# A written-out ending for the last two batches of a fused adaLN transformer block

## The reference

```python
h = layernorm(x) * (1 + ca) + sa
x = x + ga * attention(h)       # 16 heads of 64, causal softmax, out @ Wo + bo
h = layernorm(x) * (1 + cb) + sb
x = x + gb * ffn(h)             # fp4(silu(fp4(h) @ fp4(Wg).T) * (fp4(h) @ fp4(Wu).T)) @ fp4(Wd).T
```

## Time and profile before

| | |
|---|---|
| median of three runs | 1296.12 us |
| profiled execution, its own time | 1295.38 us |
| its span, first to last instruction | 1293.6 us |
| mean granted TensorE clock | 0.989 |
| PE, DVE, ACT, POOL busy, share of the span | 96%, 76%, 69%, 66% |
| PE busy in the last of 40 slices | 3 tenths (7 in the one before, 9 in all but the first) |

### The profile page before, as it was taken

How to read it: one execution, slowest core, us unless ns; L and a number is a source line. 1 busy time by engine, 2 the same in 40 slices (tenths; PEclk the granted TensorE clock), 3 DMA queues, 4 the chain that set the end, 5 groups by cost and what they waited for, 6 DMA issues and landing times.

```text
span 1293.6 us, 34330 instructions
## 1 busy us (share of the span) xinstructions
PE 1247.5 (96%) x10194; PEld 1023.9 (79%) x10194; DVE 985.3 (76%) x2461; ACT 898.1 (69%) x2988; POOL 853.9 (66%) x1595
## 2 busy tenths in 40 slices
PE   6999999999999999999999999999999999999973
PEld 4778888888888878888878888888888888888853
DVE  5577877777878777878777877777787777787863
ACT  6776776777776777766777777777677777677640
POOL 4757676667676666766666766667766666767653
PEclk9999999999999999999999999999999999999995
DMA  3000000000000000000000000000000000000000
GB/s 104 20 20 24 18 6 23 22 22 22 16 10 18 22 22 22 20 6 18 22 22 22 22 11 11 22 22 22 22 16 6 22 22 22 22 16 6 19 20 10
DMA packets 38920, 26.53 MB, mean 21 GB/s; under 512 B 2896, under 2 KB 34128, under 8 KB 38896
## 3 DMA queue, kind: packets, MB, share of 16 engines
q1 hardware_dynamic: 38480, 25.96, 7.1%
q10 hardware_dynamic: 416, 0.26, 0.1%
HBM read 21.94 MB, written 4.28 MB: 20 GB/s over the span
## 4 chain that ended last, share of the span: by engine, by line
PE 94%; DVE 2%; ACT 2%; POOL 1%; issue 1%; DMA 0%; POOLq 0%; DVEq 0%; ACTq 0%
PE ps_m L1037 25%; PE ps_s L1136 19%; PE ps_m L1011 18%; PE ps_o L1166 14%; PE ps_m L1089 9%; PE ps_s L1146 5%; PE ps_m L1113 3%; ACT probs L659 1%; ACT qk L617 0%; DVE neg_max L861 0%; POOL qy L75 0%; POOL qy L73 0%; POOL probs L451 0%; DMA x_in<-L_attn_x 0%; POOL hq L77 0%
## 5 line engine op out<-in xcount | busy, mean ns | idle before, releaser
L659 ACT ACTIVATE probs<-ps_s,neg_max 128x128 f32<-128x128 f32 (+1 forms) x1024 | 424.1, 433 | 182.1 <-PE ps_s L1146 180.5
L451 POOL TENSOR_SCALAR probs<-probs,r_den 128x256 f32<-128x256 f32 (+1 forms) x768 | 354.9, 479 | 0.0
L861 DVE TENSOR_REDUCE neg_max<-ps_s 128x4 f32<-128x1024 f32 x256 | 305.6, 1215 | 61.1 <-PE ps_s L1136 61.1
L449 POOL TENSOR_TENSOR probs<-probs,r_den 128x128 f32<-128x128 f32 x256 | 107.3, 419 | 308.0 <-DVE r_den L872 293.8
L1136 PE MATMUL ps_s<-qk 64*128 64x256 f32 x2048 | 265.0, 394 | 1.8 <-ACT probs L659 1.8
L613 ACT COPY probs_t<-ps_m 128x512 f32<-128x512 f32 x288 | 168.5, 606 | 120.8 <-PE ps_m L1011 120.6
L1011 PE MATMUL ps_m<-ident,probs 128*128 128x128 f32 x1536 | 235.8, 277 | 7.1 <-ACT qk L617 3.6
L1136 PEld LDWEIGHTS ps_s<-qk 64*128 64x128 f32 x2048 | 183.0, 187 | 61.7 <-issue 32.5
L659 ACT ACTIVATION_READ_ACCUMULATOR probs<-ps_s,neg_max 128x1 f32 x1024 | 221.0, 216 | 0.0
L1011 PEld LDWEIGHTS ps_m<-ident,probs 128*128 128x128 f32 x1536 | 172.2, 140 | 40.4 <-ACT qk L617 13.4
L1166 PE MATMUL ps_o<-probs_t,v 128*64 128x256 f32 (+1 forms) x2048 | 194.7, 332 | 3.6 <-ACT probs_t L613 1.9
(11 more groups left out here) (111 smaller groups left out, 1787.6 us busy)
## 6 DMA issues: line engine op xcount, KB each, us to landing
mod_a<-mod_rows SPq DMA_DIRECT2D x32, 256.0 KB, 3.4
x_res<-L_attn_x SPq DMA_DIRECT2D x32, 128.0 KB, 2.1
out<-y_out SPq DMA_DIRECT2D x32, 128.0 KB, 1.8
x_in<-L_attn_x SPq DMA_DIRECT2D x31, 128.0 KB, 2.1
mod_b<-mod_rows SPq DMA_DIRECT2D x32, 64.0 KB, 2.9
wkv<-L_attn_Wkv SPq DMA_DIRECT2D x3, 256.0 KB, 6.0
wo<-L_attn_Wo SPq DMA_DIRECT2D x1, 512.0 KB, 5.6
wkv<-L_attn_Wkv SPq DMA_DIRECT2D x2, 128.0 KB, 3.7
```

Of the source, the lines that this page charges most:

```text
L449: nc.gpsimd.tensor_tensor(cols, cols, r_den[:, u % 4, 0:1].to_broadcast([P, P]), ALU.mult)
L451: ins = nc.gpsimd.tensor_scalar(cols, cols, r_den[:, u % 4, s:s + 1], 1.0, ALU.mult, ALU.mult)
L659: ins = nc.scalar.activation(probs[:, u % 4, h, t * P:(1 + 2 * t) * P], ps_s[:, 2 * (u % 2) + h, t * N:t * N + (1 + t) * P], ACT.Exp, bias ...
L861: nc.vector.tensor_reduce(neg_max[:, u % 4, :], ps_s[:, 2 * (u % 2):2 * (u % 2) + 2, :].rearrange("p b (t j) -> p (b t) j", t=2), AX.X, AL ...
```

## The change

Iterations 32 and 33 are gone from PE, ACT, DVE and POOL (`for i in range(last, B)`); SP's `body` stops after 31. Behind iteration 31 each engine gets a list of its own (`LAST` = 31, `FORE` = 30). In it:

- `wo` is summed in pieces, as pairs come in: units 0 to 3 of tile 0 behind the values of pair 2, then units 0 to 5 of tile 1 and 4 to 5 of tile 0, and the last two units of each behind the copy of pair 3.
- The steps use `ps_s`, `ps_o` and `ps_m` each with a bank of its own choice.
- The high part of `xqt` is copied by ACT; DVE does the low part.
- Scale and shift (`h2a`, `h2`) of batch 31, the fp4 rounding of its input, and that of its hidden tile 1 are on DVE. POOL rounds the hidden tiles of batch 30 and tile 0 of batch 31, and makes `rstd` of batch 31 between the two tiles of batch 30.
- Batch 31's result goes to `x_in` and is stored tile by tile; its gate row comes from a tile of its own, `mod_last`, loaded early.

`shared_step` takes the destination instead of a bank number; nothing else of iterations 0 to 31 changes.

```diff
@@ sync
             iterations(sp, body, B - 2)
-            sp.wait_ge(stored, 16 * B)
+            sp.dma_start(mod_last[:, :], mod_rows[LAST, 4].partition_broadcast(P)).then_inc(mod_last_loaded, 16)
+            sp.wait_ge(down_scaled, 2 * FORE)
+            sp.dma_start(mod_b[:, :], mod_rows[FORE, 4].partition_broadcast(P)).then_inc(mod_b_loaded, 16)
+            sp.wait_ge(y_ready, 2 * LAST)
+            sp.dma_start(out_v[FORE], y_out[:, :, :]).then_inc(stored, 16)
+            for t in range(2):
+                sp.wait_ge(y_ready, 2 * LAST + t + 1)
+                sp.dma_start(out_v[LAST][:, t, :], x_in[:, t, :]).then_inc(stored, 16)
+            sp.wait_ge(stored, 16 * (B + 1))
@@ gpsimd
             iterations(pool, body)
+            normalize_unit(LAST, UNITS - 1)
...
+            round_hidden_half(FORE, 0)
+            rstd(LAST, ln2_pool, x1_steps, X1_STEPS * B, mv2, var2, rstd2)
+            round_hidden_half(FORE, 1)
+            round_hidden_half(LAST, 0)
@@ scalar
+            last_out_copy(2, ps_o[:, :])
+            last_transposed(0)
+            act.wait_ge(xqt_full, LAST)
+            nc.scalar.copy(xq_r[0][:, :], ps_m[0][:, 0:N]).then_inc(xqt_high, 1)
+            last_transposed(1)
+            last_tanh(FORE, 0, ps_s[:, 0, 0:I])
+            last_out_copy(3, ps_s[:, 3, :])
+            last_tanh(FORE, 1, ps_s[:, 2, 0:I])
+            last_hidden_copy(FORE, 0, ps_o[:, 0:IP])
+            act.wait_ge(xqt_full, B)
+            nc.scalar.copy(xq_r[0][:, :], ps_m[1][:, 0:N]).then_inc(xqt_high, 1)
+            last_tanh(LAST, 0, ps_s[:, 0, 0:I])
+            last_tanh(LAST, 1, ps_s[:, 2, 0:I])
...
@@ vector
+            last_gated(FORE, 0, ps_s[:, 0, 0:I])
+            last_hidden(FORE, 0, ps_s[:, 1, 0:I])
+            last_hidden_scales(FORE, 0)
+            last_attended(0)
+            last_attended(1)
+            dve.wait_ge(x1_steps, X1_STEPS * LAST + 2)
+            layer_norm_stats(x1, stats2, mv2, x1_steps, X1_STEPS * LAST + 2)
+            last_gated(FORE, 1, ps_s[:, 2, 0:I])
+            last_hidden(FORE, 1, ps_m[0][:, 0:I])
+            dve.wait_ge(ln2_pool, 2 * B)
+            normalized([xn2[:, t * P:t * P + P] for t in range(2)], x1, mv2, rstd2, xn2_ready)
...
+            nc.vector.tensor_tensor(h2a_v, xn2_v, both_tiles(mod_a[:, 2, :]), ALU.mult).then_inc(h2a_ready, 1)
...
+            nc.vector.tensor_tensor(h2_v, h2a_v, both_tiles(mod_a[:, 3, :]), ALU.add).then_inc(h2_ready, 1)
...
+            quantize_scales(nc, Steps(dve, xq_steps, QUANT_STEPS, LAST), h2, 2 * P // BLOCK, amax[0], scale[0], inverse[0])
+            quantize_magic(nc, Steps(dve, xq_steps, QUANT_STEPS, LAST, SCALE_STEPS), h2, 2 * P // BLOCK, inverse[0], qy[0],
+                           qm[0])
+            dve.wait_ge(xqt_full, LAST)
+            quantize_round(nc.vector, Steps(dve, xq_round, ROUND_STEPS, LAST), xq, 2 * P // BLOCK, scale[0], qy[0], qm[0])
+            last_down(FORE, 0, ps_m[2][:, 0:P], mod_b[:, :], (mod_b_loaded, 16 * LAST), x1_keep, y_out)
+            dve.wait_ge(xqt_high, 2)
+            nc.vector.tensor_tensor(xq_r[1][:, :], ps_m[1][:, 0:N], xq_r[0][:, :], ALU.subtract).then_inc(xqt_ready, 2)
+            last_hidden_scales(FORE, 1)
+            last_gated(LAST, 0, ps_s[:, 0, 0:I])
+            last_hidden(LAST, 0, ps_s[:, 1, 0:I])
+            last_hidden_scales(LAST, 0)
+            last_gated(LAST, 1, ps_s[:, 2, 0:I])
+            last_hidden(LAST, 1, ps_m[0][:, 0:I])
+            last_hidden_scales(LAST, 1)
+            dve.wait_ge(hqt_full, 2 * LAST)
+            quantize_round(nc.vector, Steps(dve, hq_round[1], ROUND_STEPS, LAST), hq[:, 1, :], I // BLOCK, scale[2], qy[2], qm[2])
+            last_down(FORE, 1, ps_o[:, 0:P], mod_b[:, :], (mod_b_loaded, 16 * LAST), x1_keep, y_out)
+            for k in range(2):
+                last_down(LAST, k, ps_s[:, k, 0:P], mod_last[:, :], (mod_last_loaded, 16), x1, x_in)
@@ tensor
+            last_values(2, ps_o)
+            shared_step("t", LAST, 9, ps_s[:, 0, :])
...
+            last_attended(0, range(0, 4))
...
+            shared_step("xqt", FORE, 0, ps_m[0])
+            shared_step("t", LAST, 10, ps_s[:, 1, :])
+            shared_step("t", LAST, 11, ps_s[:, 2, :])
...
+            shared_step("gate", FORE, 0, ps_s[:, 0, :])
...
+            shared_step("up", FORE, 0, ps_s[:, 1, :])
+            last_values(3, ps_s[:, 3, :])
...
+            last_attended(1, range(0, 6))
+            last_attended(0, range(4, 6))
+            pe.wait_ge(ot_ready, PAIRS * B)
+            last_attended(0, range(6, 8))
+            last_attended(1, range(6, 8))
+            shared_step("gate", FORE, 1, ps_s[:, 2, :])
+            shared_step("up", FORE, 1, ps_m[0])
+            shared_step("hqt", FORE, 0, ps_o)
+            pe.wait_ge(wo_scaled, 2 * B)
+            shared_step("down", FORE, 0, ps_m[2][:, 0:P])
+            shared_step("xqt", LAST, 0, ps_m[1])
... gate and up of both tiles of LAST
+            shared_step("hqt", FORE, 1, ps_s[:, 3, :])
+            shared_step("down", FORE, 1, ps_o)
+            shared_step("hqt", LAST, 0, ps_m[1])
+            pe.wait_ge(gated, 2 * LAST + 1)
+            shared_step("down", LAST, 0, ps_s[:, 0, :])
+            shared_step("hqt", LAST, 1, ps_s[:, 3, :])
+            pe.wait_ge(h_ready, 2 * LAST + 1)
+            shared_step("down", LAST, 1, ps_s[:, 1, :])
```

More of the change, by code:

```diff
@@ L145, in adaln_block @@
         mod_b = sb("mod_b", [P, P])
+        mod_last = sb("mod_last", [P, P])
         stats1 = sb("stats1", [P, 2, 6])
@@ L253, in adaln_block @@
         xqt_ready = sem("xqt_ready")
+        xqt_high = sem("xqt_high")
         tanh_ready = sem("tanh_ready")
@@ L307, in iterations @@
                 body(i)
-            for i in range(last, B + 2):
+            for i in range(last, B):
                 body(i)
@@ L372, in adaln_block @@
         POOL_SETUP = 7
+        LAST, FORE = B - 1, B - 2
+        BANK_LEFT = {}
+        for _, (kind, b, part, bank, _) in sorted(shared_steps(LAST).items()):
+            BANK_LEFT[bank] = (kind, b, part)
         block = ctx.enter_context(nc.Block())
@@ L724, in _, with last_out_copy, last_tanh, last_hidden_copy @@
             iterations(act, body)
+            def last_out_copy(pair, src):
+                act.wait_ge(o_full, PAIRS * LAST + pair + 1)
+                nc.scalar.copy(o_t[:, 2 * pair:2 * pair + 2, :], src.rearrange("p (u j) -> p u j", u=2)).then_inc(ot_ready, 1)
+            def last_tanh(b, k, src):
+                act.wait_ge(gate_full, 2 * b + k + 1)
+                act.wait_ge(gated, 2 * b + k - 1)
+                nc.scalar.activation(th[:, k, :], src, ACT.Tanh, scale=0.5).then_inc(tanh_ready, 1)
+            def last_hidden_copy(b, k, src):
+                act.wait_ge(hqt_full, 2 * b + k + 1)
+                nc.scalar.copy(hq_t[:, k, :], src).then_inc(hqt_ready, 1)
+            def last_transposed(g):
+                act.wait_ge(pt_full, 3 * PAIRS * LAST + 10 + g)
+                nc.scalar.copy(probs_t[:, 4 * g:4 * g + 4, :], ps_s[:, g, :].rearrange("p (c j) -> p c j", c=4)
+                               ).then_inc(pt_ready[g], 1)
+            last_out_copy(2, ps_o[:, :])
[11 more added lines that the diff above has]
+            last_tanh(LAST, 1, ps_s[:, 2, 0:I])
+            last_hidden_copy(FORE, 1, ps_s[:, 3, 0:IP])
+            last_hidden_copy(LAST, 0, ps_m[1][:, 0:IP])
+            last_hidden_copy(LAST, 1, ps_s[:, 3, 0:IP])
         @block.vector
@@ new lines, in last_attended @@
+            def last_attended(k):
+                dve.wait_ge(wo_full, 2 * LAST + k + 1)
+                dve.wait_ge(mod_a_loaded, 16 * B)
+                dve.wait_ge(kept, LAST)
+                nc.vector.tensor_tensor(attn[:, k, :], ps_m[1 + k][:, 0:P], mod_a[:, 0, :], ALU.mult).then_inc(wo_scaled, 1)
+                dve.wait_ge(wo_scaled, 2 * LAST + k + 1)
+                dve.wait_ge(xgb_ready, B)
+                nc.vector.tensor_tensor(x1[:, k, :], attn[:, k, :], x_gb[:, k, :], ALU.add).then_inc(x1_steps, 1)
@@ new lines, in last_down @@
+            def last_down(b, k, src, gate, loaded, kept_x, dst):
+                dve.wait_ge(down_full, 2 * b + k + 1)
+                dve.wait_ge(*loaded)
+                nc.vector.tensor_tensor(ffn[:, k, :], src, gate, ALU.mult).then_inc(down_scaled, 1)
+                dve.wait_ge(down_scaled, 2 * b + k + 1)
+                dve.wait_ge(kept, LAST)
+                dve.wait_ge(stored, 16 * FORE)
+                nc.vector.tensor_tensor(dst[:, k, :], ffn[:, k, :], kept_x[:, k, :], ALU.add).then_inc(y_ready, 1)
@@ L1237, in _, with last_values @@
             for place in ((2, 7), (3, 1), (3, 2)):
-                shared_step(*shared[place][0:4])
+                kind, b, k, bank, _ = shared[place]
+                shared_step(kind, b, k, ps_m[bank])
             iterations(pe, body)
+            def last_values(pair, dst):
+                for g in range(3):
+                    pe.wait_ge(pt_ready[g], PAIRS * LAST + pair + 1)
```

(19 more changed lines are left out.)

79 lines of the change are left out of this document (65 added, 14 removed).

## The result

The changed kernel takes 1283.5 us, the median of four runs (1283.06 to 1283.81), against 1296.14 for the kernel before (1295.63 to 1297.10): a ratio of 0.9901, 95% interval 0.9889 to 0.9912. The forecast was 1283.7. A repeat beside the last experiments gave 1283.08 (1283.01 to 1284.93).

The account below looks back on a forecast made before the run. The ending behind 1257.5 is bound by a chain of dependent steps, one engine at a time. Links laid along old times: 1291.36 - 1279.0 = 12.4 us gained, span 1281.2, profiled run 1283.0, median 1283.7; own range 1282.6 to 1285.0.

Parts of the forecast that it names:

- Start: Start of the ending, PE's values of pair 2: stays at 1243.5, as iterations 0 to 31 are untouched.
- Rival 4: Looped batches: `mod_last` shifts later SBUF tiles and slows them; from 0.44 us each the whole gain is gone; chance 0.04.
- PE up to `wo`: PE from values of pair 2: 9.1 us of work, little waiting; `wo` complete at 1252.5 and 1253.0, before 1257.71.
- Rival 2: PE ahead of `wo`: idle time of the first stretch stays, `wo` ends at 1256; +2.3, 1286.0 us; chance 0.14.
- Residual sums and statistics: DVE behind `wo`: POOL's rounding holds both residual sums, to 1253.65 and 1254.6, 0.8 lost; statistics end 1255.4.
- rstd to rounding: Batch 31's input: `rstd` 1256.5, scale and shift on DVE to 1258.05, rounding ends 1261.4; 11.0 us won so far.
- Hidden part: Batch 31's hidden tiles: DVE does batch 30 tile 1 first, to 1265.45; fp4 ends 1269.5 and 1273.6, rounding 1275.25.
- The end: Transposes 0.88, copy 0.48, last down 1.5 and DVE 0.62 us: last sum at 1279.0, before 1291.36.
- Rival 1: PE in the ending: the clock comes back to full level, saving 1.5 us, so 1282.2; chance 0.14.
- Rival 3: DVE beside POOL's roundings: POOL holds every DVE instruction that reads SBUF, some 2.6 net, 1286.3 us; chance 0.08.
- The hold: DVE instructions with two SBUF inputs, or scales on SBUF, end only behind a running POOL product; 1.4 us in all.

Follow-up runs that it names:

- the last experiments: Runs of the changed kernel plus extra matmuls on idle PE, some with `xqt` of batch 30 moved earlier; medians 1283.06, 1282.71 and 1282.53 us.
- the one profiled execution with fillers: Changed kernel plus 52 bf16 matmuls into an unused bank where PE idles; values of pair 2 to last DVE sum 34.51 us against 35.96, median 1283.06.
- the thin roundings: Changed kernel with POOL's last three roundings cut to three two-column instructions each; values of pair 2 to last DVE sum 34.27 us against 35.96.
- the kernel with batch 30 first: Changed kernel with DVE's scales and magic of batch 30 tile 1 ahead of batch 31's normalization; 1286.69 us (one run).
- the two kernels with late sums: Changed kernel with `wo` in whole sums behind pair 3, 1283.76 us; also with both roundings, scale and shift on POOL and one store, 1287.36 us.
- in the last: Changed kernel with `xqt` of batch 30 earlier and extra PE matmuls: 32, then 20 and 14, and four behind the last transposes; median 1282.53 us.

## Why the prediction was right

The time was right to 0.2 us, and partly by luck: the gain in the stretch was 11.85 us where I had 12.4. The profiled run of before lay 0.74 below its median and that of after only 0.2, and the start of the ending, which wanders by 2 us between profiles, fell within 0.02 us of the old one. The mechanism, a chain of links that the new order shortens, is what the trace shows. By steps:

- *Start.* 1243.5 as before. Rival 4, 0.44 us for each looped batch or more, did not happen.
- *PE up to `wo`.* Tile 1 complete at 1253.35, forecast 1253.0. Gate began at 1247.83, not 1247.7, since I had left out the handoff of 0.14 from the split to PE; the other 0.2 is spread over the groups behind it (gate and up took 1.13 to the next group where I had 1.05). Rival 2 (1256) did not happen. That the early units delay `xqt` was not in my list; it costs up to 0.4.
- *Residual sums and statistics.* Held by POOL as priced in kind. In size the first was 0.47 (I had 0.75), the second 0.78 (0.6 to 0.65). Last sum at 1254.82, forecast 1254.6.
- *rstd to rounding.* 1256.76, 1258.32, 1261.76; forecast 1256.5, 1258.05, 1261.4. The five moved DVE instructions took 0.42 to 0.43. The roundings on DVE and scale and shift are worth 2.12 and 0.67 by experiment, 2.3 and 0.7 by the forecast's own terms.
- *Hidden part.* First product at 1265.76, forecast 1265.45: DVE's other batch is in front of it, as said. For the holding of L55 and L62 the sum had 0.7 and 0.63 us in the two tiles, which is less than the 0.71 and 0.33, 1.04 together, that it read for the two instructions in the old trace. Measured were 0.44 and 0.48: L62 took 0.85 twice, as in the old trace, but L55 only 0.29 and 0.33, since it began just ahead of the end of a POOL product. The queue's pause of 0.1 between the two products, which I had left out, made up for part of that. Magic ends at 1273.81, forecast 1273.6.
- *The end.* 1279.49, forecast 1279.0. The terms that were too small: down takes 1.62 at the lower clock, not 1.5, and the last transposes stand behind the down of tile 0 in PE's queue (1275.71; their input was done at 1275.49).
- *Rival 1* did not happen: the second and third stretch had clocks of 0.69 and 0.50. Its price was near: the prediction has 1.5 (its four terms add up to 1.6), and the one profiled execution with fillers won 1.45, though by another sum: 0.27 on `xqt`, nothing from the gate, 0.47 up to the end of the last transposes, 0.71 on down. *Rival 3* falls with the thin roundings.
- *The hold.* By the forecast the sum would be 1.4 us lower without it; by the rows of the thin roundings it is about 1.0 on the chain, the difference lying in the holding of L55 and L62. The Trainium skill (GPSIMD Engine Reference, Key points) names two-port modes and two SBUF inputs as what contends with POOL. The two-input instructions here agree (0.29 up to 0.78, 0.52 to 0.85); L55 has one SBUF input, and no run here shows whether it is in a two-port mode.

## What to carry to other kernels

When a pipeline drains, give its last iterations lists of their own: the longest chain first in every queue, older batches in its gaps. Here that, with the banks it needs, was 8.5 of 11.85 us, more than moving work to faster engines (2.8) and splitting sums (0.5); the split store gave nothing. What the free banks alone are worth was not tried. Price a DVE instruction that is held by a running POOL product by where that product ends, and count only what the next link then really waits for. And measure an ending from a mark in its own trace, not by total time, when the part ahead of it wanders by more than the effect.

## What was not expected of the hardware

- The hold lasts until the POOL instruction has ended: a DVE sum of 128 columns ended at 1254.82, 0.14 behind POOL's product (1254.68); L62 ended at 1268.99, 0.37 behind (1268.62). In the kernel with batch 30 first, two normalizations of 0.61 grew to 2.12. In the changed kernel and that one the held instruction ended 0.14, 0.28 and 0.37 us behind POOL's at 128, 256 and 352 columns. In the other direction it showed once in each of the two kernels with late sums: a DVE sum of 0.29 began 0.03 ahead of a POOL product, which then took 1.05 instead of 0.93. That is not simply who begins first: the first of the two normalizations also began 0.05 ahead of a POOL product, and was held by it. What decides is open.
- Fillers on PE do not keep the granted clock at its upper level (2.4 GHz) by themselves: it fell to the lower one (1.2 GHz) about when 10 of them began, near 1269.5 in the first such kernel, and just behind the start of 32, near 1258.4 in the last. There it came back while they ran, near 1261.8; in the first it came back near 1272.9, with the fillers done at 1271.95.
- The size of the last store (64 or 128 KB) does not show in the 2.2 us from the last sum to the end of the span.
